# A sparse expert layer on one Trainium2 core: gate and up weights as the stationary operand, fetched per tile through a ring

## The chip, the core and the metric

The kernel runs on one core of a Trainium2 chip. Five engines work side by side, each with its own instruction stream: PE (TensorE, matrix products, with PEld for the loading of its stationary operand), DVE (VectorE), ACT (ScalarE), POOL (GpSimd) and SP (SyncE, which here only issues DMAs). They meet through semaphores. The metric is the device time of one execution in microseconds; lower is better.

## What is computed

Two transformer-like layers over `x` of shape (4, 256, 256). Each layer adds the result of an attention-like block and of an expert block. The change touches only the expert block of layer 0:

```python
x = hidden_states.reshape(-1, 256)                # 1024 tokens
probs = softmax(x @ w_router)                     # 8 experts
top_vals, top_idx = top_k(probs, 2)
for e in range(8):
    w_e = sum(where(top_idx == e, top_vals, 0))   # 0 for most tokens
    g = x @ w_gate[e] * 0.5                       # 256 x 512
    u = x @ w_up[e]                               # 256 x 512
    h = silu(g) * u @ w_down[e] * 0.25            # 512 x 256
    out = out + w_e[:, None] * h
```

## The kernel before

**The stages.** Layer 0's graph attention runs until about 235 us of the span, then the router and the sparse expert stage until about 452 us, then layer 1's graph block, its attention, and its 33 dense experts until the end.

**The sparse stage.** Each token goes to 2 of 8 experts, so there are 2048 (token, expert) rows. They are sorted by expert into tiles of 128 rows, each expert's group filled up to a multiple of 128, which makes TILES = 23 tiles at most. VectorE works out the place of each row (`slot`) and for each tile the expert that owns it, as an offset into the weights (`w_at`). POOL scatters the rows of `norm` to `x_rows` in DRAM with 16 indirect DMAs. SP waits for all of them (`rows_out`) and then loads tile after tile into `xg`, three buffers. After the last tile POOL gathers the results from `y_rows`.

**The weights.** All of gate, up and down of the 8 experts lie in `w_all`, 12.6 MB, loaded at the start of the program by 24 DMAs of 512 KB (L404 to L408). A tile's three weight blocks are addressed by a register that PE loads from `w_at` (`value_load`, L707).

**One tile on PE.** `turn_rows` (L703) transposes the 128 x 256 rows into `XB`, ACT copies them to `xgT` (L966). `gate` (L712) and `up` (L720) take `xgT` as the stationary operand and the weights as the moving one, 512 columns wide, 2 products each; the result has tokens on partitions. ACT makes `gact` = silu (L973), DVE multiplies with the up bank to `hid` (L1455). Because the down product needs the inner index on partitions, `turn_hidden` (L729) transposes `hid` in 4 blocks and ACT copies them to `hgT` (L979). `down` (L737) is 4 products with 256 moving columns. ACT copies the result to `yg` (L985), SP stores it (L460). Products are in float32, of which the trace shows two PE records for each product and one for each transpose.

**The order.** It is written out by hand. In iteration j PE runs gate(j), turn_hidden(j-1), up(j), turn_rows(j+1), down(j-1). On SP the order is store_rows(j), then load_rows(j+3), so that the rows of tile j+3 are fetched only once the result of tile j is copied. DVE uses the time between its products for the top-k search of layer 1's graph block (`keep_top`, L1438 to L1443), 4 steps for each tile. PE's sequencer handles its instructions in order and hands the products to a queue in front of the array; records of that sequencer are shown as PEldq.

Of the kernel before, what the change touches and what calls it, by code (L numbers as in the profile page):

```python
# [14 lines left out]
P = 128  # L15
B, N, D = 4, 256, 256
# [19 lines left out]
O_RING = 6  # L36

# [3 lines left out]
WROW = 3 * GU  # L41
# [54 lines left out]
def build(nc, x, ctxT, W0, W1, a_self0, a_neigh0, a_self1, a_neigh1, b01,  # L96
          w_router, w_gate, w_up, w_down, WqT, WkT, gamma, ln1, ln2, Wq, Wk, Wv, Wo, Wr, ebias,
          Wg, Wu, Wd, ident_in, ind_in, rope_q, rope_k, causal_in, before_in, out):
    with ExitStack() as ctx:
# [88 lines left out]
        w_all = sb_early("w_all", [P, E0, 3, GU])  # L188
# [17 lines left out]
        hgT = sb_sparse("hgT", [P, 2, I0 // P, P])  # L206
# [10 lines left out]
        w_at = sb_sparse("w_at", [P, TILES], I32)  # L217
        last = sb_sparse("last", [P, 2, T])
# [22 lines left out]
        def sb_resting(name, shape):  # L241
# [26 lines left out]
            "x_in", "const_in", "gat_in", "sim_in", "w_all_in", "before_in",  # L268
# [10 lines left out]
            "hid_turned", "hgT_copied", "y_ready", "y_copied", "tok_added", "sig_kept",  # L279
# [99 lines left out]
        def _(sp):  # L379
# [23 lines left out]
            for e in range(E0):  # L403
                sp.dma_start(w_all[:, e, 0, :].rearrange("p (c n) -> p c n", c=HC),  # L404
                             w_gate[e].rearrange("(c p) n -> p c n", p=P)).then_inc(S["w_all_in"], 16)
                sp.dma_start(w_all[:, e, 1, :].rearrange("p (c n) -> p c n", c=HC),
                             w_up[e].rearrange("(c p) n -> p c n", p=P)).then_inc(S["w_all_in"], 16)
                sp.dma_start(w_all[:, e, 2, :].rearrange("p (c n) -> p c n", c=I0 // P),  # L408
                             w_down[e].rearrange("(c p) n -> p c n", p=P)).then_inc(S["w_all_in"], 16)
# [82 lines left out]
        def _(pe):  # L492
# [200 lines left out]
            def sparse_mixture():  # L693
                GB, UB, XB, HB, YB = bank[0:2], bank[2:4], bank[4], bank[5], bank[6:8]
                flat_w = w_all[:].rearrange("p e m n -> p (e m n)")
                ats = {}

                def turn_rows(j):
                    pe.wait_ge(S[f"xg_in{j % 3}"], 16 * (j // 3 + 1))
                    if j >= 2:  # L700
                        pe.wait_ge(S["xgT_copied"], j - 1)
                    for c in range(HC):
                        mm = pe.transpose(XB[:, j % 2 * D + c * P:j % 2 * D + c * P + P], xg[:, j % 3, c * P:c * P + P], ident[:])  # L703
                    mm.then_inc(S["xg_turned"], 1)

                def gate(j):
                    ats[j] = pe.value_load(w_at[0:1, j:j + 1], min_val=0, max_val=(E0 - 1) * WROW)  # L707
                    pe.wait_ge(S["xgT_copied"], j + 1)
                    if j >= 2:
                        pe.wait_ge(S["gact_done"], j - 1)  # L710
                    for c in range(HC):
                        mm = pe.matmul(GB[j % 2][:], xgT[:, j % 2, c, :], flat_w[:, bass.ds(ats[j] + c * I0, I0)],  # L712
                                       start=c == 0, stop=c == HC - 1)
                    mm.then_inc(S["gate_ready"], 1)

                def up(j):
                    if j >= 2:
                        pe.wait_ge(S["hid_done"], j - 1)
                    for c in range(HC):
                        mm = pe.matmul(UB[j % 2][:], xgT[:, j % 2, c, :], flat_w[:, bass.ds(ats[j] + (GU + c * I0), I0)],  # L720
                                       start=c == 0, stop=c == HC - 1)
                    mm.then_inc(S["up_ready"], 1)

                def turn_hidden(j):
                    pe.wait_ge(S["hid_done"], j + 1)
                    if j >= 1:
                        pe.wait_ge(S["hgT_copied"], j)
                    for c in range(I0 // P):
                        mm = pe.transpose(HB[:, c * P:c * P + P], hid[:, j % 2, c * P:c * P + P], ident[:])  # L729
                    mm.then_inc(S["hid_turned"], 1)  # L730

                def down(j):
                    pe.wait_ge(S["hgT_copied"], j + 1)
                    if j >= 2:
                        pe.wait_ge(S["y_copied"], j - 1)
                    for c in range(I0 // P):
                        mm = pe.matmul(YB[j % 2][:, 0:D], hgT[:, j % 2, c, :], flat_w[:, bass.ds(ats[j] + (2 * GU + c * D), D)],  # L737
                                       start=c == 0, stop=c == I0 // P - 1)
                    mm.then_inc(S["y_ready"], 1)

                pe.wait_ge(S["w_all_in"], 16 * 3 * E0)
                pe.wait_ge(S["owner_done"], 1)
                turn_rows(0)
                for j in range(TILES + 1):
                    if j < TILES:
                        gate(j)
                    if j >= 1:
                        turn_hidden(j - 1)
                    if j < TILES:
# [120 lines left out]
        def _(act):  # L870
# [88 lines left out]
            def sparse_mixture():  # L959
                GB, XB, HB, YB = bank[0:2], bank[4], bank[5], bank[6:8]  # L960
# [14 lines left out]
                def copy_hidden(j):  # L975
                    act.wait_ge(S["hid_turned"], j + 1)
                    if j >= 2:
                        act.wait_ge(S["y_ready"], j - 1)
                    act.activation(hgT[:, j % 2].rearrange("p c n -> p (c n)"), HB[:], ACT.Copy).then_inc(S["hgT_copied"], 1)  # L979

# [7 lines left out]
                for j in range(TILES + 1):  # L988
                    if j < TILES:
                        gates(j)  # L990
                    if j >= 1:
# [242 lines left out]
        def _(dve):  # L1234
# [131 lines left out]
            def router0():  # L1366
# [42 lines left out]
                dve.tensor_scalar(w_at[:], owner[:], float(E0 - 1), float(WROW), ALU.min, ALU.mult).then_inc(S["owner_done"], 1)  # L1409
# [36 lines left out]
            def sparse_mixture():  # L1446
# [3 lines left out]
                for j in range(TILES):  # L1450
                    dve.wait_ge(S["gact_done"], j + 1)
                    dve.wait_ge(S["up_ready"], j + 1)
                    if j >= 2:
                        dve.wait_ge(S["hid_turned"], j - 1)
# [316 lines left out]
```

## Time and profile before

| | us |
|---|---|
| median of 3 runs | 1225.0 (1222.7 to 1226.8) |
| the profiled execution | 1225.96 |
| its span, first to last instruction | 1223.9 |
| outside the span | 2.1 |
| PE busy in the span | 1072.3 (88%) |
| DVE busy | 874.4 (71%) |
| ACT busy | 592.0 (48%) |
| POOL busy | 379.0 (31%) |
| mean granted TensorE clock | 0.906 of 2.4 GHz |

"Busy" is a mean over stages with different limits. For this change the stretch from 287.8 us (first product of the sparse stage) to 427.5 us (its last result copied) matters.

### The profile page before, as it was taken

What the parts mean: (1) busy time and instruction counts of PE and PEld (TensorE: products, weight loads), DVE (VectorE), ACT (ScalarE), POOL (GpSimd) and SP (SyncE); (2) the same over time, 40 slices, a digit from 0 to 9 for tenths busy, and PEclk for the clock granted to TensorE, in tenths of its full rate; (3) what the DMA queues carried; (4) which work ended last, traced back from release to release, by engine and by line L of the source; (5) the groups of instructions that cost most, each with busy time, mean ns of one, the idle gap of its engine ahead of it and who ended that gap; (6) DMA issues with size and microseconds to landing.
All of it is one profiled execution on the core that took longest, in us unless ns stands there. A gap on an engine that the chain in (4) does not pass through costs nothing.

```text
span 1223.9 us, 20173 instructions
## 1 busy us (share of the span) xinstructions
PE 1072.3 (88%) x6074; PEld 865.3 (71%) x6074; DVE 874.4 (71%) x2600; ACT 592.0 (48%) x1547; POOL 379.0 (31%) x315
## 2 busy tenths in 40 slices
PE   7988889535999903699999999999997999999998
PEld 3555555332666602599999999999996888888887
DVE  4787776732777348777777777777776887887887
ACT  4656465301333311577777777877775222222221
POOL 0756465122000052433333323322211233233231
PEclk9978776757999955899999999999997999999999
DMA  7900000101111131010101101000000111111111
GB/s 235 363 1 2 1 1 1 63 35 57 43 44 52 36 107 39 24 50 6 36 5 40 36 1 32 2 1 1 2 2 15 51 51 39 51 51 39 51 51 35
DMA packets 55568, 53.56 MB, mean 44 GB/s; under 512 B 5520, under 2 KB 48976, under 8 KB 55488
## 3 DMA queue, kind: packets, MB, share of 16 engines
q1 hardware_dynamic: 53952, 48.38, 12.6%
q0 software_dynamic: 1536, 4.20, 1.1%
q8 instruction: 40, 0.66, 0.2%
q14 instruction: 40, 0.33, 0.1%
HBM read 43.38 MB, written 9.18 MB: 43 GB/s over the span
## 4 chain that ended last, share of the span: by engine, by line
PE 78%; DVE 8%; issue 6%; ACT 4%; POOL 2%; DMA 1%; SPq 1%; DVEq 0%; ACTq 0%; POOLq 0%
PE bank L56 12%; PE bank L57 12%; PE bank L58 12%; PE bank L802 7%; PE bank L823 5%; PE bank L581 4%; PE bank L712 3%; PE bank L812 3%; PE bank L737 3%; PE bank L720 3%; PE bank L564 2%; PE bank L824 2%; DVE g_scale L1319 2%; PE bank L550 2%; PE bank L781 1%
## 5 line engine op out<-in xcount | busy, mean ns | idle before, releaser
L1216 POOL TENSOR_TENSOR rot_s<-swap,rq 128x512 f32<-128x512 f32 x64 | 89.2, 1394 | 196.4 <-ACT swap L1034 196.4
L952 ACT ACTIVATE silu<-bank 128x512 f32<-128x512 f32 x66 | 39.4, 598 | 177.9 <-PE bank L58 177.9
L1643 DVE TENSOR_TENSOR o_ring<-bank,o_ring 128x256 fp32r<-128x256 f32 x128 | 54.3, 424 | 93.6 <-ACT o_ring L1063 92.9
L1047 ACT ACTIVATE prob<-prob,pmin 128x128 f32<-128x128 f32 (+1 forms) x256 | 113.1, 445 | 3.6 <-DVE pmin L1624 3.6
L802 PE MATMUL bank<-kv,norm 128*128 128x128 f32 (+1 forms) x512 | 106.8, 332 | 3.2 <-DVE norm L1617 3.2
L1513 DVE SCALAR_TENSOR_TENSOR xs<-bank,wt,xs 128x256 f32<-128x256 f32 x264 | 109.1, 476 | 0.0
L1162 POOL TENSOR_TENSOR gate_r<-gate_w,gate_r 128x256 fp32r<-128x256 f32 x33 | 38.8, 1175 | 221.5 <-ACT gate_r L938 221.5
L1144 POOL TENSOR_SCALAR rest<-alpha 128x512 f32<-128x512 f32 x32 | 69.3, 2164 | 78.6 <-ACT alpha L884 77.2
L1063 ACT ACTIVATE o_ring<-bank 128x256 fp32r<-128x256 f32 x128 | 48.3, 378 | 82.1 <-PE bank L824 82.0
L56 PE MATMUL bank<-wo_r,o_ring 128*128 128x256 f32 x256 | 84.1, 328 | 0.0
L1624 DVE CUSTOM_DVE_ANT_0 prob<-bank,causal 128x128 f32<-128x128 f32 (+1 forms) x256 | 80.2, 350 | 0.8 <-PE bank L802 0.8
L1636 DVE TENSOR_SCALAR prob<-prob,pinv 128x128 f32<-128x128 f32 (+1 forms) x256 | 76.0, 339 | 4.6
L1492 DVE TENSOR_TENSOR hidf<-silu,bank 128x512 f32<-128x512 f32 x66 | 45.4, 688 | 45.9 <-ACT silu L952 43.6
L823 PE MATMUL bank<-probT,kv 128*128 128x256 f32 x256 | 76.9, 382 | 0.7 <-DVE o_ring L1643 0.7
L56 PE MATMUL bank<-down_r,hidT 128*128 128x256 f32 x264 | 74.7, 283 | 2.0 <-DVE hidT L1497 2.0
L58 PE MATMUL bank<-down_r,hidT 128*128 128x256 f32 x264 | 74.7, 283 | 0.0
L57 PE MATMUL bank<-down_r,hidT 128*128 128x256 f32 x264 | 74.7, 283 | 0.0
L1301 DVE CUSTOM_DVE_ANT_0 alpha<-alpha,norm 128x256 f32<-128x256 f32 x128 | 62.0, 521 | 17.3 <-POOL alpha L1147 16.8
L564 PE MATMUL bank<-ident,alpha 128*128 128x128 f32 x256 | 50.9, 333 | 25.0 <-ACT alphaT L903 14.1
L58 PE MATMUL bank<-wo_r,o_ring 128*128 128x256 f32 x256 | 72.3, 282 | 0.0
L57 PE MATMUL bank<-wo_r,o_ring 128*128 128x256 f32 x256 | 72.2, 282 | 0.0
L802 PEld LDWEIGHTS bank<-kv,norm 128*128 128x128 f32 x512 | 68.8, 195 | 4.0 <-DVE norm L1617 3.6
(240 smaller groups left out, 3116.3 us busy)
## 6 DMA issues: line engine op xcount, KB each, us to landing
gate_w<-in_Wg SPq DMA_DIRECT2D x33, 128.0 KB, 2.1
up_w<-in_Wu SPq DMA_DIRECT2D x33, 128.0 KB, 2.3
down_w<-in_Wd SPq DMA_DIRECT2D x33, 128.0 KB, 2.3
w_all<-in_w_gate SPq DMA_DIRECT2D x8, 512.0 KB, 10.3
w_all<-in_w_up SPq DMA_DIRECT2D x8, 512.0 KB, 10.3
w_all<-in_w_down SPq DMA_DIRECT2D x8, 512.0 KB, 10.3
wq_g<-in_Wq SPq DMA_DIRECT2D x4, 1024.0 KB, 5.0
wo_g<-in_Wo SPq DMA_DIRECT2D x4, 1024.0 KB, 5.4
```

The costliest lines, as they stand in the source:

```text
L56: pe.matmul(out, lhs[0], rhs[0], start=first, stop=False)
L57: pe.matmul(out, lhs[0], rhs[1], start=False, stop=False)
L58: return pe.matmul(out, lhs[1], rhs[0], start=False, stop=last)
L564: mm = pe.transpose(PTB[k % 2][:, mc * N + nt * P:mc * N + nt * P + P], alpha[:, k % RING, nt * N + mc * P:nt * N + mc * P + P], ident[:])
L802: mm = pe.matmul(S_BANK[u % 2][:, nt * P:nt * P + (nt + 1) * P], qT[:, (u // 2) % 4, b2 * N + nt * P:b2 * N + nt * P + P], kT[:, b * N:b * ...
L823: pe.matmul(O_BANK[:, 0:N], vt[:, t, :], probT[:, u % 2, 0:N], start=True, stop=False)
L1047: ins = act.activation(prob[:, u % 4, nt * P:nt * P + (nt + 1) * P], prob[:, u % 4, nt * P:nt * P + (nt + 1) * P], ACT.Exp, bias=pmin[:, u ...
L1144: pool.tensor_scalar(rest[:], alpha[:, k % RING, :], 1.0 / NEG - 1.0, 0.0, ALU.mult, ALU.min).then_inc(S["z_rest"], 1)
L1216: pool.tensor_tensor(rot_s[:, m % 2].rearrange("p (b n) -> p b n", b=2), swap[:, m % 2].rearrange("p (b n) -> p b n", b=2), bcast(tab[:, 1 ...
L1513: ins = dve.scalar_tensor_tensor(xs[:, t, :], DB[2 * (mod % 2) + j // 2][:, j % 2 * D:j % 2 * D + D], w, xs[:, t, :], ALU.mult, ALU.add)
L1624: ins = dve.tensor_tensor_reduce(out=prob[:, u % 4, nt * P:nt * P + (nt + 1) * P], in0=S_BANK[u % 2][:, nt * P:nt * P + (nt + 1) * P], in1 ...
L1636: ins = dve.tensor_scalar(prob[:, u % 4, nt * P:nt * P + (nt + 1) * P], prob[:, u % 4, nt * P:nt * P + (nt + 1) * P], pinv[:, u % 4, nt:nt ...
```

## The change

It turns the roles in gate and up round: blocks of 128 x 128 of the weights are stationary and `xgT` moves, 128 columns wide. The result then has the inner index on partitions, and `hid` can be the stationary operand of down as it is. `turn_hidden`, `copy_hidden` and `hgT` go. Only the down weights stay resident (`w_out`, 8 DMAs of 512 KB at the start); the gate and up weights of a tile's expert are fetched by two DMAs of 512 KB into a ring of three (`w_in`), by the new `load_inner` on SP, with the expert's number read from `e_at`.

```diff
+            def load_inner(j):
+                e = sp.value_load(e_at[0:1, j:j + 1], min_val=0, max_val=E0 - 1)
+                if j >= W_RING:
+                    sp.wait_ge(S["up_ready"], j - W_RING + 1)
+                for m, w in enumerate((w_gate, w_up)):
+                    sp.dma_start(w_in[:, j % W_RING, m, :].rearrange("p (c n) -> p c n", c=HC),
+                                 w[bass.ds(e, 1)].rearrange("e (c p) n -> p (e c) n", p=P)
+                                 ).then_inc(S[f"w_in{j % W_RING}"], 16)
+
+            sp.wait_ge(S["owner_done"], 1)
+            for j in range(W_RING):
+                load_inner(j)
             sp.wait_ge(S["rows_out"], 16 * K0 * T)
             for j in range(3):
                 load_rows(j)
             for j in range(TILES):
+                if j + W_RING < TILES:
+                    load_inner(j + W_RING)
                 store_rows(j)
                 if j + 3 < TILES:
                     load_rows(j + 3)
...
+                def inner(dst, j, m):
+                    for i in range(I0 // P):
+                        for c in range(HC):
+                            mm = pe.matmul(dst[:, i * P:i * P + P], w_in[:, j % W_RING, m, c * I0 + i * P:c * I0 + i * P + P],
+                                           xgT[:, j % 2, c, :], start=c == 0, stop=c == HC - 1)
+                    return mm
...
                 def gate(j):
-                    ats[j] = pe.value_load(w_at[0:1, j:j + 1], min_val=0, max_val=(E0 - 1) * WROW)
+                    pe.wait_ge(S[f"w_in{j % W_RING}"], 32 * (j // W_RING + 1))
                     pe.wait_ge(S["xgT_copied"], j + 1)
...
+                def down(j):
                     pe.wait_ge(S["hid_done"], j + 1)
-                    if j >= 1:
-                        pe.wait_ge(S["hgT_copied"], j)
-                    for c in range(I0 // P):
-                        mm = pe.transpose(HB[:, c * P:c * P + P], hid[:, j % 2, c * P:c * P + P], ident[:])
-                    mm.then_inc(S["hid_turned"], 1)
-
-                def down(j):
-                    pe.wait_ge(S["hgT_copied"], j + 1)
                     if j >= 2:
                         pe.wait_ge(S["y_copied"], j - 1)
-                    for c in range(I0 // P):
-                        mm = pe.matmul(YB[j % 2][:, 0:D], hgT[:, j % 2, c, :], flat_w[:, bass.ds(ats[j] + (2 * GU + c * D), D)],
-                                       start=c == 0, stop=c == I0 // P - 1)
+                    at = pe.value_load(w_at[0:1, j:j + 1], min_val=0, max_val=(E0 - 1) * GU)
+                    for i in range(I0 // P):
+                        mm = pe.matmul(YB[j % 2][:, 0:D], hid[:, j % 2, i * P:i * P + P], flat_w[:, bass.ds(at + i * D, D)],
+                                       start=i == 0, stop=i == I0 // P - 1)
                     mm.then_inc(S["y_ready"], 1)
...
-                pe.wait_ge(S["w_all_in"], 16 * 3 * E0)
+                pe.wait_ge(S["w_out_in"], 16 * E0)
...
-                    if j >= 1:
-                        copy_hidden(j - 1)
```

VectorE gets one instruction more, which writes `e_at` just before `w_at`, and its wait for `hid_turned` becomes one for `y_ready`.

PE, one iteration of the sparse stage before. A row is an instruction with its tiles; `ISA` rows compute register addresses, `TENSOR_LOAD` is the `value_load`.

```order
L707 TENSOR_LOAD w_at
L707 ISA x2
L712 ISA
L712 MATMUL bank<-w_all,xgT 128x512
L712 ISA
L712 MATMUL bank<-w_all,xgT 128x512
L729 MATMUL bank<-ident,hid 128x128 x4
L720 ISA
L720 MATMUL bank<-w_all,xgT 128x512
L720 ISA
L720 MATMUL bank<-w_all,xgT 128x512
L703 MATMUL bank<-ident,xg 128x128 x2
```

The same iteration of PE in the changed kernel (L721 is gate and up, L714 turn_rows, L743 down).

```order
L721 MATMUL bank<-xgT,w_in 128x128 x16
L714 MATMUL bank<-ident,xg 128x128 x2
L741 TENSOR_LOAD w_at
L741 ISA x2
L743 ISA
L743 MATMUL bank<-w_out,hid 128x256
```

The register load stood at the head of gate, right behind down(j-2) in program order. It now stands between the transposes of the new rows and down.

SP, the queue of DMAs in the stage, before and (below) in the changed kernel.

```order
L443 DMA wv_g<-in_Wv 128x2x128
L456 DMA xg<-x_rows 128x256 [waits rows_out]
L456 DMA xg<-x_rows 128x256 x2
L460 DMA y_rows<-yg 128x256 [waits y_copied]
L456 DMA xg<-x_rows 128x256 [waits xg_turned]
```

In the changed kernel L453 loads the rows, L457 stores the result, L465 loads the weights.

```order
L461 TENSOR_LOAD e_at
L461 ISA x2
L465 ISA [waits up_ready]
L465 DMA w_in<-in_w_gate 128x2x512
L465 DMA w_in<-in_w_up 128x2x512
L457 DMA y_rows<-yg 128x256 [waits y_copied]
L453 DMA xg<-x_rows 128x256 [waits xg_turned]
```

Between the load of one tile's rows and the store of the next result SP now also issues 1 MB of weights.

## Rows read from the trace of the kernel before

**Rows 1.** Busy time by stretch: the warm sparse stage, early weight loading (clock, DMA share, GB/s last).

```profile
core 0: us, PE busy (x) PEld busy (x) DVE busy (x) ACT busy (x) POOL busy (x), PEclk, DMA share, GB/s
295.70:423.80 128.10, 128.03 (x484) 79.26 (x485) 88.58 (x263) 39.98 (x86) 0.00 (x0) 1.00 0.14 43
30.00:40.00 10.00, 9.16 (x28) 5.81 (x28) 7.69 (x23) 7.44 (x14) 9.51 (x7) 1.00 1.07 374
```

**Rows 2.** Timeline of PE over one tile: start us, length us, records.

```profile
342.43 1.88 PE L712 MATMUL bank<-w_all,xgT 128*128 x4
344.14 0.60 PE L729 MATMUL bank<-ident,hid 128*128 128x128 f32 x4
344.58 1.88 PE L720 MATMUL bank<-w_all,xgT 128*128 x4
346.30 0.38 PE L703 MATMUL bank<-ident,xg 128*128 128x128 f32 x2
346.52 1.89 PE L737 MATMUL bank<-w_all,hgT 128*128 x8
348.25 1.88 PE L712 MATMUL bank<-w_all,xgT 128*128 x4
```

**Rows 3.** Timeline of PE and PEld around 848 us, float32 products with 128 moving columns.

```profile
847.71 1.95 PE L781 MATMUL bank<-wv_g,actT 128*128 128x128 f32 x16
849.50 0.60 PE L823 MATMUL bank<-probT,kv 128*128 128x256 f32 x2
...
847.50 1.97 PEld L781 LDWEIGHTS bank<-wv_g,actT 128*128 128x128 f32 x16
```

**Rows 4.** Timeline of ACT and SP in the same tile as rows 2, and SP one tile on.

```profile
342.63 0.38 ACT L985 ACTIVATE yg<-bank 128x256 f32<-128x256 f32 x1 [1.34 <-PE bank L737]
...
343.04 0.32 SPq L460 DMA_DIRECT2D y_rows<-yg  x1
343.40 0.43 SPq L456 DMA_DIRECT2D xg<-x_rows  x1
348.86 0.32 SPq L460 DMA_DIRECT2D y_rows<-yg  x1
349.22 1.10 SPq L456 DMA_DIRECT2D xg<-x_rows  x1
```

**Rows 5.** By tile: landing of the xg loads (23), then PE's sequencer in one tile.

```profile
DMA to landing us min/median/max: 2.1/2.2/2.7
...
L735 PEldq EVENT_SEMAPHORE  x1: 51/51/51, 345.6 to 345.6; - x1
```

**Rows 6.** PE's sequencer around the register load of one tile: duration ns, first and last start.

```profile
L707 PEldq TENSOR_LOAD <-w_at x1: 302/302/302, 340.5 to 340.5; - x1
L707 PEldq FUSED_REGOPS  x1: 151/151/151, 340.9 to 340.9; - x1
L707 PEldq SEQ_ASSERT  x1: 18/18/18, 341.1 to 341.1; - x1
...
L710 PEldq EVENT_SEMAPHORE  x1: 51/51/51, 341.2 to 341.2; - x1
```

**Rows 7.** DMA issues: out<-in engine op xcount, KB each, median us to landing.

```profile
wq_g<-in_Wq SPq DMA_DIRECT2D x4, 1024.0 KB, 5.0
```

**Rows 8.** Timeline of the last tile's end.

```profile
421.96 1.89 PE L737 MATMUL bank<-w_all,hgT 128*128 x8
422.22 0.69 DVE L1455 TENSOR_TENSOR hid<-gact,bank 128x512 f32<-128x512 f32 x1 [5.13 <-PE bank L720]
423.69 0.60 PE L729 MATMUL bank<-ident,hid 128*128 128x128 f32 x4
425.06 1.99 PE L737 MATMUL bank<-w_all,hgT 128*128 x8 [0.77 <-ACT hgT L979]
426.88 0.60 PE L764 MATMUL bank<-ident,kv 128*128 128x128 f32 x4
```

**Rows 9.** Timeline of the stage's start and, later, 128 moving columns at half clock.

```profile
289.02 3.78 PE L712 MATMUL bank<-w_all,xgT 128*128 x4 [0.56 <-ACT xgT L966]
292.59 2.41 PE L720 MATMUL bank<-w_all,xgT 128*128 x4
...
485.35 3.38 PE L781 MATMUL bank<-wv_g,actT 128*128 128x128 f32 x16 [0.81 <-ACT actT L1010]
```

**Rows 10.** Timeline: DVE's product and ACT's copy in one tile; POOL's first and last scatter.

```profile
340.85 0.69 DVE L1455 TENSOR_TENSOR hid<-gact,bank 128x512 f32<-128x512 f32 x1 [1.12 <-PE bank L720]
...
263.75 1.22 POOL L1176 DMA_INDIRECT x_rows<-norm,slot  x1 [43.33 <-DVE slot L1405]
...
283.00 0.96 POOL L1176 DMA_INDIRECT x_rows<-norm,slot  x1 [0.30 <-issue]
```

More of the change, by code:

```diff
@@ L36 @@
 O_RING = 6
+W_RING = 3
 SLOTS = B * N * K0
@@ L187, in build @@
         g_pos = sb_early("g_pos", [P, 2, N])
-        w_all = sb_early("w_all", [P, E0, 3, GU])
+        w_out = sb_early("w_out", [P, E0, GU])
+        w_in = sb_early("w_in", [P, W_RING, 2, GU])
         early.close()
@@ L217, in build @@
         w_at = sb_sparse("w_at", [P, TILES], I32)
+        e_at = sb_sparse("e_at", [P, TILES], I32)
         last = sb_sparse("last", [P, 2, T])
@@ L403, in _ @@
             for e in range(E0):
[L404 to L409, printed above, removed]
+                sp.dma_start(w_out[:, e, :].rearrange("p (c n) -> p c n", c=I0 // P),
+                             w_down[e].rearrange("(c p) n -> p c n", p=P)).then_inc(S["w_out_in"], 16)
             def load_expert(which, e, par):
@@ L693, in sparse_mixture @@
             def sparse_mixture():
-                GB, UB, XB, HB, YB = bank[0:2], bank[2:4], bank[4], bank[5], bank[6:8]
-                flat_w = w_all[:].rearrange("p e m n -> p (e m n)")
-                ats = {}
+                GB, UB, XB, YB = bank[0:2], bank[2:4], bank[4], bank[6:8]
+                flat_w = w_out[:].rearrange("p e n -> p (e n)")
                 def turn_rows(j):
@@ L710, in gate @@
                         pe.wait_ge(S["gact_done"], j - 1)
[L711 to L714, printed above, removed]
+                    inner(GB[j % 2], j, 0).then_inc(S["gate_ready"], 1)
                 def up(j):
@@ L718, in up @@
                         pe.wait_ge(S["hid_done"], j - 1)
[L719 to L724, printed above, removed]
-                    pe.wait_ge(S["hid_done"], j + 1)
-                    if j >= 1:
-                        pe.wait_ge(S["hgT_copied"], j)
-                    for c in range(I0 // P):
-                        mm = pe.transpose(HB[:, c * P:c * P + P], hid[:, j % 2, c * P:c * P + P], ident[:])
-                    mm.then_inc(S["hid_turned"], 1)
-                def down(j):
-                    pe.wait_ge(S["hgT_copied"], j + 1)
+                    inner(UB[j % 2], j, 1).then_inc(S["up_ready"], 1)
+                def down(j):
+                    pe.wait_ge(S["hid_done"], j + 1)
                     if j >= 2:
                         pe.wait_ge(S["y_copied"], j - 1)
-                    for c in range(I0 // P):
-                        mm = pe.matmul(YB[j % 2][:, 0:D], hgT[:, j % 2, c, :], flat_w[:, bass.ds(ats[j] + (2 * GU + c * D), D)],
-                                       start=c == 0, stop=c == I0 // P - 1)
+                    at = pe.value_load(w_at[0:1, j:j + 1], min_val=0, max_val=(E0 - 1) * GU)
+                    for i in range(I0 // P):
+                        mm = pe.matmul(YB[j % 2][:, 0:D], hid[:, j % 2, i * P:i * P + P], flat_w[:, bass.ds(at + i * D, D)],
+                                       start=i == 0, stop=i == I0 // P - 1)
                     mm.then_inc(S["y_ready"], 1)
-                pe.wait_ge(S["w_all_in"], 16 * 3 * E0)
+                pe.wait_ge(S["w_out_in"], 16 * E0)
                 pe.wait_ge(S["owner_done"], 1)
@@ L746, in sparse_mixture @@
                         gate(j)
-                    if j >= 1:
-                        turn_hidden(j - 1)
-                    if j < TILES:
                         up(j)
@@ L959, in sparse_mixture @@
             def sparse_mixture():
[L960 removed]
+                GB, XB, YB = bank[0:2], bank[4], bank[6:8]
                 def copy_rows(j):
@@ L973, in gates @@
                     act.activation(gact[:, j % 2, :], GB[j % 2][:], ACT.Silu, scale=0.5).then_inc(S["gact_done"], 1)
[L975 to L979, printed above, removed]
                 def copy_out(j):
@@ L1408, in router0 @@
                 chain.link(dve.tensor_reduce(owner[:], ends[:], X, ALU.add))
-                dve.tensor_scalar(w_at[:], owner[:], float(E0 - 1), float(WROW), ALU.min, ALU.mult).then_inc(S["owner_done"], 1)
+                dve.tensor_scalar(e_at[:], owner[:], float(E0 - 1), None, ALU.min)
+                dve.tensor_scalar(w_at[:], owner[:], float(E0 - 1), float(GU), ALU.min, ALU.mult).then_inc(S["owner_done"], 1)
                 for k, test in enumerate((ALU.is_equal, ALU.not_equal)):
```

9 lines of the change are left out of this document (3 added, 6 removed).

## The prediction

> **What bounds the kernel now.** I read the busy shares by stretch first, then PE's timeline over one tile, then what ACT, SP and PE's sequencer do in that tile. From 295.7 to 423.8 us PE is busy 128.03 of 128.10 us at the full granted clock, 2.4 GHz [rows 1]: the sparse stage is bound by PE, without gaps. Taking start to start, one tile is gate 1.71, turn_hidden 0.44, up 1.72, turn_rows 0.22 and down 1.73 us, together 5.82 [rows 2]. Everything else fits under that. DVE and ACT have idle time before each tile's work (1.12 us before the product, 1.34 before the copy) [rows 4, 10]. The DMAs use 0.14 of their time [rows 1]. But one loop is nearly as long as PE's. The rows of tile j+3 are asked for only when the result of tile j is copied. In the tile that starts at 342.43 the copy runs from 342.63, the store is issued at 343.04, the rows' load at 343.40 [rows 2, 4]. With a landing of 2.2 us that is 345.6, and at 345.6 PE's sequencer is at L735, the first instruction behind the transposes that need these rows [rows 5]. I read this as the sequencer having stood at the wait for that DMA. PE itself reaches the transposes at 346.30 [rows 2], so the cover is 0.7 us.
>
> **The change, part by part.**
>
> Gate and up. Each was 2 products of 512 columns and becomes 8 of 128, the same columns in all. The nearest row is L781, float32, 128 moving columns, a new stationary block for each record: 16 records from 847.71 to the next product at 849.50, 0.112 us each [rows 3]. A product is two records, so gate takes 16 x 0.112 = 1.79 us and up the same, +0.15 us a tile for both.
>
> Here a rule of the Trainium skill speaks against the change. The row says that 16 loads take 1.97 us beside 16 products that take 1.95 [rows 3]: the loads run under the products. The page "TensorE: Matmul & The Clock Gate", Part 3, says that a weight load overlaps a product in flight only if it goes to other row groups, and these blocks use all rows; its Part 2 also allows a load into a background buffer. If loads were added to products, the case is rival D.
>
> turn_hidden and copy_hidden. 4 transposes go, -0.44 us of PE a tile [rows 2]. ACT loses a 0.6 us copy that nobody waited for, except at the end.
>
> PE's own sum is then 1.79 + 1.79 + 0.22 + 1.73 = 5.53 us a tile, 0.29 less than 5.82. If that were all, 22 tiles would give -6.4 us.
>
> The register load. It moves from the head of gate, where 1.73 us of queued down products covered it, to between turn_rows and down. So it now stands behind the wait for the DMA, where the cover is gone. From its start to the next instruction of the sequencer is 340.5 to 341.2, 0.7 us [rows 6]. With about 0.1 us for the semaphore instruction before it and 0.1 for the address and first block after it, down's first product can start 0.9 us after the rows land. Counted from the start of gate: rows land at 345.6 - 342.43 = 3.17, down can start at 3.17 + 0.9 = 4.07. PE would be ready for it at 1.79 + 1.79 + 0.22 = 3.80, so it idles 0.27 us. Restarted after such a gap, 8 down records take 425.06 to 426.88, 1.82 us [rows 8]. The tile takes 4.07 + 1.82 = 5.89 us, and the next copy, store and load hang on its end: the round result, copy, store, load, sequencer, down is the new bound, 0.07 us longer than PE's 5.82 before. This holds for the iterations 2 to 21, in which the rows come by that round: 20 x 0.07 = +1.4 us.
>
> The own size of the register load is a second place for the skill. The row has 302 ns for the load alone [rows 6]. The page "DMA: Bandwidth & Descriptors", Latency and other measured facts, gives a floor of about 600 ns for it. By the page each tile would be 0.3 us longer and the sum 6 us higher; the trace does not agree here, and its duration is used.
>
> The late issue. One rows' load of the 21 in the loop took 1.10 us to issue instead of 0.43 (at 349.22) [rows 4]. The cover took it before; now it lands in full: +0.6 us. SP issues twice as many DMAs, and such an issue may come oftener, up to three times, +1.2 more at the upper bound.
>
> The 1 MB of weights a tile. Behind the rows' load, SP is free at 1.40 us after the start of gate (343.40 + 0.43). Its register load is 0.8 us by the same rows [rows 6]; the two DMAs start to issue at 2.2. A DMA of 1 MB lands 5.0 us after its issue [rows 7], so this lands at 7.2, that is 1.3 us into the next tile, and is wanted more than one tile later. Its data stop moving some time before that landing. The next store is issued at 0.6 and the next rows' load at 1.0 into that tile, and a load of 128 KB needs 2.2 us of which little is data, at 374 GB/s (1 MB in 2.8 us) [rows 1, 5]. So I take no delay. The bounds are zero and half of the 1 MB still ahead of the rows, 1.4 us a tile; nearest to zero because the transfer has 5.9 us for 2.8 us of work. The range keeps a part of it. A gain from it is excluded, since nothing waited for these weights.
>
> The start. `load_inner` for tiles 0 to 2 waits for `owner_done`, which comes near the first scatter at 263.75; the last scatter is issued at 283.00 [rows 10]. 3 MB are 8.4 us, done before. VectorE's additional instruction stands behind `slot_done`, on which the scatters hang, so it costs nothing. At half clock 16 records of 128 columns take 3.38 us (ends included), gate's four before took 3.57 start to start [rows 9]: even. The down weights still come in long before. The 8 MB less at the start had no one waiting.
>
> The ends. Iterations 1 and 22 lose the 0.29 us: -0.6. After the last down-but-one, PE turned `hid`, waited for ACT's copy and started down at 425.06, 1.37 us after 423.69 [rows 8]. Now `hid` is ready at 422.22 + 0.69 = 422.91, the register load and address make it 423.8, against 423.69: about 0.15 of the 1.37 stays, and with the restart at 0.1 the gain is -1.1 us.
>
> Sum: +1.4 + 0.6 - 0.6 - 1.1 = +0.3 us. The profiled execution had 1225.96, which gives 1226.3; the median of the runs is 1.0 below it, which gives 1225.3.
>
> **The rivals.**
>
> B, the register load stays covered. If the sequencer does not stand at the DMA's wait but runs on (L735 at 345.6 would then be chance), or rows land 0.3 us earlier than I read, PE's 5.53 holds: 22 x -0.29 - 1.1 = -7.5 us, 1217.5. For it: the queue before PE is evidently long, since the sequencer is at L707 at 340.5, nearly 2 us before gate starts. Against it: the agreement of landing and L735.
>
> C, the weights stand before the rows in the DMA engines. In place is SP's one queue: the 1 MB of one tile is issued before the next store and rows' load. It decides once the last bytes of the 1 MB move later than about 2 us into the next tile; my reckoning has them end at about 1. Each 0.1 us past that costs 2 us in all, since the round has no cover left. With 0.4 us a tile the time is 1225.3 + 8 = 1233; with the full 1.4 us it is 1253. For it: the round is now the bound, so every delay of issue or landing counts, and landings went up to 2.7 us even with an idle queue [rows 5]. The slower register load belongs here by its size.
>
> D, weight loads are not hidden for 128 columns: each record costs 0.112 more, 32 x 0.112 x 23 = +82 us, 1307. The row of L781 speaks against it [rows 3].
>
> That the new form leaves PE with the old 5.82 because it does not do what it says is excluded by the instruction order.
>
> **How the numbers follow.** Within 0.3% (3.7 us, about what a measurement of this kernel can tell from no change) around 1225.0 is my forecast, the round as the bound: 0.53, its own range 1222 to 1229. B, faster by more than 0.3%: 0.18. C, slower: 0.27; D: 0.02. Predicted is 1225.3. The range reaches down to B's 1217 and up to 1236, which leaves out the larger half of C's sizes and D, about 0.15. Faster 0.18, same 0.53, slower 0.29.
>
> **What would show it.** In the changed kernel's profile: L721 records 0.112 us apart at full clock (right), 0.2 and more (D). Start of gate to start of gate 5.9 us with a gap of about 0.3 us on PE before each down, from tile 2 on (right); 5.5 without gap (B); 6.2 and more with xg landings above 2.4 us (C). The sequencer's register load should start at the landing of xg. The gap between the last two downs shrinks from 1.4 us to about 0.2. If the store or rows' load is issued later than 0.6 and 1.0 us after the start of gate, SP's queue was the error. It would be wrong altogether if the granted clock fell in the stage because of the gaps, which no row suggests.

## The result and the profile after

The changed kernel takes 1231.9 us (median of 8 runs, 1228.6 to 1232.7) against 1225.9 for the kernel before in the same session: ratio 1.0050, 95% interval 1.0035 to 1.0064. It is slower, by 6 us. The prediction said 1225.3, "within 0.3%" as the likeliest case; the time lies inside the whole range given (1217 to 1236) and outside the likeliest case's own range (1222 to 1229). The profiled execution took 1230.93 us against 1225.96, so the profile shows 5.0 of the 6 us.

The busy time by stretch comes first, as in [rows 1]; the columns are the same.

```profile
core 0: us, PE busy (x) PEld busy (x) DVE busy (x) ACT busy (x) POOL busy (x), PEclk, DMA share, GB/s
295.70:426.80 131.10, 125.41 (x911) 115.32 (x910) 87.17 (x259) 29.23 (x64) 0.00 (x0) 1.00 0.59 202
310.00:410.00 100.00, 94.95 (x680) 86.52 (x680) 70.58 (x210) 22.20 (x49) 0.00 (x0) 1.00 0.63 214
```

Before, PE was busy 128.03 of 128.10 us. Now it idles 5.7 us of 131.1, at the same full clock, and the DMAs carry 202 GB/s instead of 43. PE is no longer the bound. Why the idle time is there shows in two kinds of tile. The first kind is the tile forecast: PE's timeline over tile and end of stage (it answers to [rows 2] and [rows 8]), SP's timeline in the same tile, and then the register loads of PE's sequencer (ns min/median/max).

```profile
417.22 3.73 PE L721 MATMUL bank<-xgT,w_in 128*128 128x128 f32 x32
420.80 0.38 PE L714 MATMUL bank<-ident,xg 128*128 128x128 f32 x2
421.29 1.99 PE L743 MATMUL bank<-w_out,hid 128*128 x8
423.12 3.73 PE L721 MATMUL bank<-xgT,w_in 128*128 128x128 f32 x32
426.69 3.71 PE L743 MATMUL bank<-w_out,hid 128*128 x16
430.24 0.60 PE L767 MATMUL bank<-ident,kv 128*128 128x128 f32 x4
...
417.83 0.34 SPq L457 DMA_DIRECT2D y_rows<-yg  x1
418.23 0.42 SPq L453 DMA_DIRECT2D xg<-x_rows  x1
...
L741 PEldq TENSOR_LOAD <-w_at x23: 295/302/506, 296.9 to 427.7; - x23
```

Gate and up together are 3.58 us, the rows' load is issued 1.01 us after the start of gate, and down starts at 4.07 us, although the transposes were done at 3.80. The tile takes 5.90 us. These are the prediction's 3.58, 1.0, 4.07, 3.80 and 5.89.

The second kind was not forecast at this frequency. PE's timeline of the tile that starts at 342.50, then SP's. Brackets hold the idle time before a row and what ended it.

```profile
342.50 3.73 PE L721 MATMUL bank<-xgT,w_in 128*128 128x128 f32 x32
346.45 0.44 PE L714 MATMUL bank<-ident,xg 128*128 128x128 f32 x2 [0.21 <-DMA xg<-x_rows]
347.31 1.99 PE L743 MATMUL bank<-w_out,hid 128*128 x8 [0.42 <-issue]
349.13 3.73 PE L721 MATMUL bank<-xgT,w_in 128*128 128x128 f32 x32
355.23 3.73 PE L721 MATMUL bank<-xgT,w_in 128*128 128x128 f32 x32
...
343.11 0.34 SPq L457 DMA_DIRECT2D y_rows<-yg  x1
343.51 1.38 SPq L453 DMA_DIRECT2D xg<-x_rows  x1
345.63 0.40 SPq L465 DMA_DIRECT2D w_in<-in_w_gate  x1
346.13 0.41 SPq L465 DMA_DIRECT2D w_in<-in_w_up  x1
349.74 0.34 SPq L457 DMA_DIRECT2D y_rows<-yg  x1
350.14 0.43 SPq L453 DMA_DIRECT2D xg<-x_rows  x1
```

The rows' load starts on time, 1.01 us after gate, but takes 1.38 us to issue instead of 0.43. The rows land 2.9 us after the start of the issue instead of 2.2, so 0.7 us late; PE waits first for them and then for its sequencer, and the tile takes 6.63 us. The tile behind it, 349.13 to 355.23, still has 6.10. The tile view of xg gives the issue over all tiles (ns min/median/max) and the landing:

```profile
L453 SPq DMA_DIRECT2D xg<-x_rows x23: 343/425/1386, 284.7 to 418.2; - x23
...
DMA to landing us min/median/max: 2.0/2.2/3.1
```

Of the 20 periods of the loop, six hold such an issue (0.9 to 1.39 us): 6.59, 6.63, 6.51, 6.88, 6.54 and 6.21 us, and two stand behind one (6.10 and 6.37). The others lie between 5.81 and 5.96.

What stands beside the late issues is in the view of the DMA queues (packets, MB, share of 16 engines over the stretch). The first stretch is 343.2 to 343.8, around the late issue. The second is the 0.4 us before the one late issue of the kernel before, at 349.22 [rows 4].

```profile
q1 hardware_dynamic: 24, 0.03, 13.2%
q8 instruction: 1, 0.02, 12.5%
```

```profile
q8 instruction: 1, 0.02, 19.4%
```

Queue q8 fetches instructions, 16 KB in one packet. They are PE's: in a run below, 45 more instructions on PE moved four of the seven fetches in the loop one tile ahead. 12.5% of 16 engines over 0.6 us is 1.2 us for the packet. In the trace of the changed kernel each of the six late rows' loads (and a weights' load of 1.30 us at 309.2) has such a fetch beside it and is released about 0.4 us after the fetch ends. Fetches come every 13 to 19 us instead of every 23 to 29, since a tile now has 42 product records on PE and had 22. The experiments ask how much each of these two findings, the bare round and the late issue, is worth.

The stage was also measured alone, from the start of the first gate product to the first transpose behind the last down:

| kernel | stage, us | against before | rest of the span behind it |
|---|---|---|---|
| before | 137.86 | | 797.0 |
| after | 142.16 | +4.3 | 798.9 |
| after, again | 144.31 | +6.5 | 796.7 |
| after with 45 more PE instructions ahead | 143.23 | +5.4 | 798.3 |
| early register load | 134.10 | −3.8 | 796.6 |
| rows first | 130.15 | −7.7 | 797.1 |
| both | 129.92 | −7.9 | 798.0 |
| no reload of weights | 139.41 | +1.6 | 799.0 |
| half of the weights | 138.43 | +0.6 | 796.2 |
| two register loads | 153.65 | +15.8 | 798.1 |
| products of before, weights by ring | 138.48 | +0.6 | 799.5 |
| before with rows first | 137.98 | +0.1 | 797.1 |

The last column moves over 3.3 us in no relation to the edits, so what one profile shows behind the stage (+1.9 here) is scatter of single executions. The stage column carries the argument, but it scatters too: two profiles of the changed kernel differ by 2.1 us. The medians of the runs agree with the column to within about 2 us. One run of the kernel with the products of before and weights by ring took 1442.2 us and is left out of its median.

### The profile page after: what moved, and what is told of

Read it like the earlier page. It is cut to its first block, busy times and chain, and to the rows that moved or that the text cites. A ratio compares the mean times of both kernels' runs of the same rounds, so it can differ in the third digit from the quotient of the medians.

```text
span 1229.1 us, 21098 instructions
## 1 busy us (share of the span) xinstructions
PE 1073.5 (87%) x6526; PEld 908.1 (74%) x6534; DVE 874.6 (71%) x2601; ACT 580.7 (47%) x1524; POOL 379.6 (31%) x315
## 4 chain that ended last, share of the span: by engine, by line
PE 78%; DVE 9%; issue 4%; ACT 4%; DMA 2%; POOL 2%; SPq 1%; DVEq 0%; ACTq 0%; POOLq 0%
PE bank L56 13%; PE bank L57 12%; PE bank L58 12%; PE bank L805 7%; PE bank L721 6%; PE bank L826 4%; PE bank L593 4%; PE bank L743 4%; PE bank L815 3%; PE bank L576 2%; PE bank L827 2%; DVE g_scale L1314 2%; PE bank L562 2%; PE bank L784 1%; POOL ytok L1179 1%
## 5 line engine op out<-in xcount | busy, mean ns | idle before, releaser
L721 PEld LDWEIGHTS bank<-xgT,w_in 128*128 128x128 f32 x736 | 87.9, 196 | 2.8 <-issue 1.7
L721 PE MATMUL bank<-xgT,w_in 128*128 128x128 f32 x736 | 88.3, 280 | 1.1 <-ACT xgT L969 1.1
L56 PE MATMUL bank<-wo_r,o_ring 128*128 128x256 f32 x256 | 84.2, 329 | 0.0
L58 PE MATMUL bank<-wo_r,o_ring 128*128 128x256 f32 x256 | 72.3, 283 | 0.0
```

What stands on the lines that cost most here:

```text
L56: pe.matmul(out, lhs[0], rhs[0], start=first, stop=False)
L58: return pe.matmul(out, lhs[1], rhs[0], start=False, stop=last)
L721: mm = pe.matmul(dst[:, i * P:i * P + P], w_in[:, j % W_RING, m, c * I0 + i * P:c * I0 + i * P + P], xgT[:, j % 2, c, :], start=c == 0, st ...
```

## The experiments

Each was timed beside the kernel before; times are medians, ratios are against the kernel before with their 95% intervals. The kernel before had medians of 1225.1, 1225.7 and 1224.9 us in the three sessions; a ratio can differ by 0.001 from that of two medians.

**The register load back ahead of gate.**

```diff
 def gate(j):
+    ats[j] = pe.value_load(w_at[0:1, j:j + 1], ...)
     pe.wait_ge(S[f"w_in{j % W_RING}"], 32 * (j // W_RING + 1))
 ...
 def down(j):
-    at = pe.value_load(w_at[0:1, j:j + 1], ...)
+    at = ats[j]
```

> The changed kernel with one thing moved: PE's register load for down (302 ns, 0.7 us with what follows it) stands at the head of gate again, as in the kernel before. Theory (the round result, copy, store, rows' load, register load, down closes the loop): down can start as soon as the rows have landed and the transposes are done, so a tile takes PE's own 3.57 + 0.22 + 1.72 = about 5.55 us instead of 5.89, there is no gap before down except in tiles whose rows' load is issued late, and the time falls by about 20 x 0.34 = 7 us against the changed kernel, plus some 2 us of late issues that the regained 0.3 us of cover take: 1222 to 1225. Rival (the 1 MB of weights a tile is what slows the rows): the gaps stay, 1230 to 1232.

Measured 1221.4 us, 0.9960 (0.9943 to 0.9977). PE's timeline has both kinds of tile again:

```profile
367.03 0.44 PE L715 MATMUL bank<-ident,xg 128*128 128x128 f32 x2 [0.52 <-DMA xg<-x_rows]
367.30 1.92 PE L745 MATMUL bank<-w_out,hid 128*128 x8
369.06 3.73 PE L722 MATMUL bank<-xgT,w_in 128*128 128x128 f32 x32
372.63 0.38 PE L715 MATMUL bank<-ident,xg 128*128 128x128 f32 x2
372.85 1.89 PE L745 MATMUL bank<-w_out,hid 128*128 x8
374.58 3.73 PE L722 MATMUL bank<-xgT,w_in 128*128 128x128 f32 x32
```

369.06 to 374.58 is 5.52 us with PE never idle: the new products are 0.3 us a tile cheaper, once the register load is covered. 13 of 20 tiles are so. Where the rows' load is issued late (up to 1.60 us here), PE still waits for the rows, 0.5 us in the tile shown. The place of the register load is therefore worth 8 us of stage in the profiles and about 10 us by the medians, a little more than expected, and the late issues survive.

**Rows before result on SP.**

```diff
     load_inner(j + W_RING)
-store_rows(j)
 if j + 3 < TILES:
     load_rows(j + 3)
+store_rows(j)
```

> The changed kernel with SP's order turned: the rows of tile j+3 are loaded before the result of tile j is stored, so that they no longer wait for its copy. The register load stays where the change put it. Theory (the round through SP is the bound): the rows are there a tile ahead, PE's sequencer never stands at their wait, the register load is hidden by the queued products, every tile takes about 5.55 us, and the late issues no longer reach PE: against the changed kernel -7 us for the gaps and -5 us for the late issues, 1218 to 1220. Rival (the register load costs PE its 0.7 us wherever it stands before down): the tile stays at 5.8 or more, 1228 and above.

Measured 1217.9 us, 0.9929 (0.9904 to 0.9954), faster than both kernels by more than the intervals, and with the next run the fastest of all. Busy time in the middle of the stage, then PE's and SP's timeline:

```profile
310.00:410.00 100.00, 100.00 (x765) 96.29 (x764) 75.84 (x226) 24.98 (x55) 0.00 (x0) 1.00 0.68 238
...
368.99 3.73 PE L721 MATMUL bank<-xgT,w_in 128*128 128x128 f32 x32
374.51 3.73 PE L721 MATMUL bank<-xgT,w_in 128*128 128x128 f32 x32
...
366.16 0.46 SPq L453 DMA_DIRECT2D xg<-x_rows  x1
369.60 0.34 SPq L457 DMA_DIRECT2D y_rows<-yg  x1
370.70 0.95 SPq L465 DMA_DIRECT2D w_in<-in_w_gate  x1
371.75 0.41 SPq L465 DMA_DIRECT2D w_in<-in_w_up  x1
372.22 0.46 SPq L453 DMA_DIRECT2D xg<-x_rows  x1
```

The rows' load no longer waits for the result's copy, so there is no round. It is issued right behind the 1 MB of weights and lands only after 4.3 us (median; 5.0 at most), twice as long as before, and nobody waits: all tiles are 5.52 us. Late issues are there too (0.95 us at 370.70 is one), and cost nothing. The stage is 7.7 us shorter than before; rival B of the prediction had priced exactly this state, PE's own sum, at 7.5.

**Both edits.** 

> The changed kernel with both corrections, the register load at the head of gate and the rows' load ahead of the store. Theory: with the rows first PE has no gap left (5.52 us a tile in all 20), so the register load's place is worth nothing more: the same as e2, 1217 to 1219, ratio to the kernel before 0.991 to 0.995. Rival (the register load still costs PE something): 1 us or more below e2.

Measured 1218.8 us, 0.9945 (0.9924 to 0.9966), stage 129.92 against 130.15. The second edit adds nothing to the first: with rows early, the register load is covered again where it stands.

**The same order in the kernel before.** The two lines on SP exchanged in the kernel before. 

> The kernel before with SP's order turned as in e2: rows of tile j+3 loaded before the result of tile j is stored. Theory: PE had no gaps there, so nothing changes, 1224.5 to 1226, ratio 0.999 to 1.001. Rival (the earlier loads help by themselves, so that the gain of e2 is not the form of the products): 1222 or less.

Measured 1226.4 us, 0.9999 (0.9983 to 1.0016); all tiles 5.82, PE busy 100.00 of 100 us. The time is 0.4 us above the range expected, the ratio inside it. The kernel before gains nothing from it, since PE bounded it. The gain of the kernel above is that of the change, freed of its round.

**Two register loads.**

```diff
+pe.value_load(w_at[0:1, j:j + 1], ...)
 at = pe.value_load(w_at[0:1, j:j + 1], ...)
```

> The changed kernel with PE's register load in front of down done twice. Theory (it stands bare between the landing of the rows and down): the second one adds its full 0.65 to 0.7 us to each of the 20 tiles in the loop, +13 to +14 us against the changed kernel, 1244 to 1246, and the tile's period goes from 5.9 to 6.55. Rival (it is covered and something else makes the gap): no more than 2 us are added.

Measured 1242.5 us, 1.0139 (1.0111 to 1.0167).

```profile
368.01 3.73 PE L721 MATMUL bank<-xgT,w_in 128*128 128x128 f32 x32
371.58 0.38 PE L714 MATMUL bank<-ident,xg 128*128 128x128 f32 x2
372.91 1.99 PE L744 MATMUL bank<-w_out,hid 128*128 x8 [0.95 <-issue]
374.74 3.73 PE L721 MATMUL bank<-xgT,w_in 128*128 128x128 f32 x32
```

Down now starts 4.90 us after gate instead of 4.07, and most tiles take 6.6 us, 0.7 more than the 5.9. That shows each register load bare on the round, at the 0.7 us of [rows 6]. The total is 1.5 us under the range expected, and only one late issue (0.94 us) is in this profile, although the same 1 MB of weights moves in every tile. The tile is 0.7 us longer, so the weights' bytes end earlier against the next gate. Here is q8 from 327.7 to 328.1 in the tile that starts at 327.80, then the rows' load:

```profile
q8 instruction: 1, 0.02, 16.1%
...
328.80 0.42 SPq L453 DMA_DIRECT2D xg<-x_rows  x1
```

The fetch starts with gate and takes 1.0 us, where six of the seven in the changed kernel's loop start 0.6 to 1.1 us behind it. Five of the seven fetches in the loop lie so, from 0.2 us before gate to 0.1 behind it, and delay the rows' load by at most 0.1 us. Of the other two, one makes the late issue, and the other starts 0.4 us behind the issue of a load that then landed after 2.8 us (its tile took 7.25).

**No weights in the loop.** The tiles from the fourth on use the weights of the first three.

```diff
-if j + W_RING < TILES:
-    load_inner(j + W_RING)
 store_rows(j)
 ...
-pe.wait_ge(S[f"w_in{j % W_RING}"], 32 * (j // W_RING + 1))
+pe.wait_ge(S[f"w_in{j % W_RING}"], 32)
```

> The changed kernel without the weight loads of tiles 3 to 22: the ring keeps the weights of the first three tiles, so most tiles are computed with another tile's gate and up weights; all instructions of PE, ACT and DVE are the same. It takes away 20 MB of traffic and 40 DMAs from SP's queue. Theory A (the late issues of the rows' load in 6 of 20 tiles come from the fetch of PE's instructions, 16 KB at a time, which starts within 0.5 us of each of them): they stay, and the time is that of the changed kernel, 1230 to 1232. Theory B (they come from the weights' descriptors in the same queue, or from their bytes still moving): they go, the tiles take 5.9 us throughout, 4 to 5 us less, 1226 to 1228.

Measured 1226.8 us, 1.0005 (0.9987 to 1.0024). My theory had expected 1230 to 1232, with the late issues still there. It fell; the rival's number came.

```profile
366.09 3.73 PE L719 MATMUL bank<-xgT,w_in 128*128 128x128 f32 x32
372.00 3.73 PE L719 MATMUL bank<-xgT,w_in 128*128 128x128 f32 x32
376.00 0.44 PE L712 MATMUL bank<-ident,xg 128*128 128x128 f32 x2 [0.26 <-DMA xg<-x_rows]
...
372.62 0.32 SPq L457 DMA_DIRECT2D y_rows<-yg  x1
372.98 1.35 SPq L453 DMA_DIRECT2D xg<-x_rows  x1
```

366.09 to 372.00 is 5.91 us: the round is as long without any traffic of weights, so it is made of waits and not of contention. But only two of 20 tiles suffer now (6.71 and 6.67): the one shown, and one whose load was issued in time and landed after 3.0 us, with a fetch that started 0.6 us behind it. PE's instructions are as many as in the changed kernel, and the fetches too. What differs is their place in the tile: five of the seven in the loop begin 0.7 to 1.0 us before the result's store is issued, and are over when the rows' load is. In the changed kernel six of them begin between 0.04 us before and 0.45 us after the store's issue, and are in the way of the rows' load.

**The products of the kernel before, with the weights fetched for each tile.**

```diff
-for i in range(I0 // P):
-    for c in range(HC):
-        mm = pe.matmul(dst[:, i * P:i * P + P], w_in[...], xgT[:, j % 2, c, :], ...)
+for c in range(HC):
+    mm = pe.matmul(GB[j % 2][:], xgT[:, j % 2, c, :], w_in[:, j % 3, 0, c * I0:c * I0 + I0], ...)
 ...
+turn_hidden(j - 1)
```

> The kernel before with the ring alone: gate and up weights are fetched per tile as in the change, but they move and xgT is stationary as before, with turn_hidden, and the register load at the head of gate. Theory (the traffic itself costs nothing; what costs is the lost cover): a tile takes 5.82 us, as before, and longer only where a rows' load is issued more than 0.7 us late, 0 to 2 us in all: 1225 to 1228. Rival (1 MB a tile delays the rows or slows PE's reads): 1230 and above.

Measured 1226.9 us, 0.9997 (0.9978 to 1.0016). The issues of rows reach 1.61 us here too, and five in the loop are late (0.79 us and more), but most of this is covered: three tiles have 6.10, 6.37 and 5.94 us and the others 5.82. In the profile the DMA ring alone costs 0.6 us of stage. Weights, fetches and late issues do harm only by what goes beyond the cover of the round.

**The changed kernel again, and with 45 more instructions on PE ahead of the stage.** The added instructions only raise a semaphore; they shift the boundaries of the 16 KB blocks to other instructions.

```diff
+for _ in range(45):
+    pe.sem_inc(S["pe_held"])
 pe.wait_ge(S["w_out_in"], 16 * E0)
```

> The changed kernel itself once more, on the same chip as the next three, so that they have it beside them. Both theories: 1230 to 1232 where the kernel before has 1225 to 1226, and the same 6 or 7 late issues, since the fetches of PE's instructions stand at fixed places of its program.

> The changed kernel with 45 semaphore increments more in PE's program, just before the sparse stage, where PE waits anyway; everything else is the same, the 1 MB of weights a tile too. It moves every later 16 KB piece of PE's instructions by 45 instructions, about half a tile. Theory A (the rows' load is issued late when it falls into the fetch of such a piece): the fetches fall elsewhere in the tile, late issues go from 7 to 3 or fewer in the profile, and the time falls by 2 to 4 us against the changed kernel, with the other tiles still at 5.9. Theory B (late issues come from the weights' traffic): 6 or 7 late issues and no change.

Measured 1232.1 us, 1.0043 (1.0026 to 1.0060), and 1232.1 us, 1.0046 (1.0028 to 1.0063). The first profile has seven late issues in the loop. The second has six, and a seventh load that was issued in time and landed after 3.2 us, with a fetch 0.5 us behind it. Four of the seven fetches fall one tile earlier with the added instructions, but again behind the start of gate, by 0.4 to 0.8 us (one by 1.5) against 0.5 to 1.0. So the place of a block's end among the instructions doesn't decide where in the tile a fetch runs; the expectation that the shift would change the number of late tiles fell.

**Half of the weights.** Only the gate weights are fetched, and up computes with them too. The DMA wait takes half the count.

```diff
-for m, w in enumerate((w_gate, w_up)):
+for m, w in enumerate((w_gate,)):
```

> The changed kernel with only the gate weights fetched, 512 KB a tile instead of 1 MB; up is computed with the gate weights too, by the same instructions. The padded run left the fetches of PE's instructions at the same time of the tile, 0.6 to 1.0 us after the start of gate, which is when the weights' bytes end; with no weights at all the fetches came 0.1 to 0.4 us before it. Theory C (such a fetch is asked for a little before the start of gate and stands behind the weights' bytes; it then falls on the rows' load that SP issues at 1.0): with half of the bytes, which end some 1.4 us earlier, the fetches start near -0.4 again, at most 2 rows' loads are issued late, and the time is that of the run without weights, 1226 to 1228. Rival D (the number of DMAs or any traffic at all is what counts): 5 to 7 late issues as before, 1230 to 1232, or in between in proportion.

Measured 1225.4 us, 1.0003 (0.9981 to 1.0026). First q8 in the stretch from 324.1 to 324.5, then PE and SP there:

```profile
q8 instruction: 1, 0.02, 15.1%
```

```profile
324.42 3.73 PE L721 MATMUL bank<-xgT,w_in 128*128 128x128 f32 x32
...
325.03 0.32 SPq L457 DMA_DIRECT2D y_rows<-yg  x1
325.39 0.43 SPq L453 DMA_DIRECT2D xg<-x_rows  x1
```

The fetch takes 15.1% of 16 x 0.4 us, 1.0 us, and starts ahead of gate. The rows' load that follows at 325.39 is issued in 0.43 us. In the changed kernel, the tile that starts at 324.16 has its fetch start at 324.9 and its rows' load take 1.16 us. With half the bytes one rows' load in the loop is late by much (1.50 us) where six were, and its stage is 3.7 us shorter. The time is a little under the range expected. From none to half the traffic changes little (139.4, 138.4), from half to all it costs 4 to 6 us, by either profile of the changed kernel. The amount of traffic alone is not what decides, since two register loads left all of it in place and had one late issue; both runs fit with the time at which the bytes end. In the changed kernel the 2 KB packets of the weights still move in the first 0.7 us of gate:

```profile
q1 hardware_dynamic: 117, 0.24, 101.6%
```

That is the stretch from 349.2 to 349.8, right behind the start of gate at 349.13: 117 packets, all but one of 2 KB, and the engines full. From 349.9 on they are nearly empty. I read it so that a fetch that was due in this time runs behind these bytes, at 0.6 to 1.1 us, and there meets the rows' load. Two times in each kernel bear on it. Both are medians, in us from the start of gate: the end of the last 2 KB packet, over 19 tiles, and the start of the fetch, over the fetches in the loop (seven; five in the last kernel).

| kernel | ordinary tile, us | bytes end | fetch starts |
|---|---|---|---|
| no reload of weights | 5.9 | none | −0.2 |
| half of the weights | 5.9 | −0.45 | −0.1 |
| two register loads | 6.6 | 0.2 | 0.0 |
| after | 5.9 | 0.9 | 0.8 |
| early register load | 5.52 | 1.3 | 1.1 |
| after, again | 5.85 | 0.9 | 0.8 |
| after with 45 more PE instructions ahead | 5.9 | 0.8 | 0.7 |
| rows first | 5.52 | 0.7 | 1.0 |
| products of before, weights by ring | 5.82 | 1.25 | 0.8 |

The first five rows rise together; the last two do not lie on their line, so the end of the bytes is not all that sets the start of a fetch.

All twelve profiles together say more about the fetch and the issue. 59 loads on SP, of rows or weights, were issued from 0.2 us before a fetch to its end; 58 were released between 0.27 and 0.44 us after the fetch's end, nearly all at 0.37, whether the issue took 0.4 or 1.5 us in all. Of the 550 other loads in the stage two took more than 0.5 us, and one of these was issued 0.2 us before a fetch. The 38 stores that met a fetch took no more than 0.34 us.

## Why the prediction was right, and where it was wrong

| term of the sum | forecast, us | measured in the profile, us |
|---|---|---|
| 20 tiles, the round as bound | +1.4 | +1.5 |
| late issues of the rows' load | +0.6 (up to +1.8) | +4.7 |
| first and last tiles | −1.7 | −1.9 |
| stage | +0.3 | +4.3 |

The time forecast was 6.6 us too low. The whole range held because it kept room for rival C, whose mechanism is not the one that came; that part is luck.

**What bounds the kernel.** Right. The reading that PE's sequencer stood at the rows' DMA with 0.7 us of cover left [rows 5] carried the forecast. Moving the register load behind that wait used the cover up: 5.52 us a tile when it is ahead of gate, 5.90 behind the wait, 6.6 when it is doubled.

**Gate and up.** Right: 3.58 us for both, 0.112 us a record, as L781 had shown [rows 3]. The weight loads are hidden, against what Part 3 of the Trainium skill's page "TensorE: Matmul & The Clock Gate" would give for blocks that use all rows; rival D is out.

**The round.** Right to 0.01 us in the tile at 417.22, by each step. The twelve ordinary tiles take 5.895 us on average, which over 20 is +1.5 us. Rival B's condition, a covered register load, did not hold, and its price was confirmed by rows first (−7.7 us against −7.5).

**The register load's own time.** 302 ns, median of 23, as in [rows 6], and not the 600 ns that the Trainium skill gives on "DMA: Bandwidth & Descriptors", Latency and other measured facts. Two register loads showed that its whole price is the 0.7 us with the address behind it.

**The late issue.** This is the term that was mis-sized. The prediction took one in 21 (the loop has 20 such loads), put at 0.6 us, and up to three times as many, because SP issues twice as many DMAs. Six came, at 0.3 to 1.0 us each, with 0.2 and 0.5 us in two tiles behind them, together +4.7 us. The reasoning had the wrong cause: not SP's number of DMAs, which was as large with two register loads and one late issue, but the fetches of PE's instructions, more of them and later in the tile. They stand beside every late issue, in the kernel before too. The prediction never asked what ran in the DMA queues at 349.22 [rows 4], and took the one late issue for chance.

**The 1 MB of weights.** Half right. The rows were not behind the weights: where their load is issued in time in the loop, it lands after 2.1 to 2.4 us, and did after 2.1 to 2.3 before. The engines are full with their bytes until 0.7 us into the next tile, about where the prediction had them end, and not past the 2 us that rival C needed. C's sign, tiles of 6.2 us and more with landings above 2.4, did show in the six tiles with a late issue; the sign could not tell a late issue from a slow transfer. But the sum took the effect of the traffic as zero, and taking it away or halving it gave 3 to 6 us of stage back. By the reading above it works through something that the prediction did not name: it pushes the fetches of instructions onto the rows' load. C's price of 1233 was near the result for another reason.

**The ends and the start.** Right in sum. From the start of the last down that has no cover to the next transpose it was 4.92 us before (421.96 to 426.88, [rows 8]) and is 3.55 now (426.69 to 430.24): −1.37, for which −1.1 was forecast. The rest of the first and last tiles gave −0.5 for −0.6.

**The chances.** The round without cover was known, and each 0.1 us of further delay priced at 2 us; a resource that was seen once and not explained deserved more than 0.6 us with that price. "Slower" had 0.29 and should have had more than "same".

**What stays open.** That the fetch holds the issue rests on the constant distance between the ends of the two in twelve profiles; no run changes the fetch alone. That the weights' bytes push the fetch back rests on the runs in which the bytes end earlier or later, by less traffic or by a longer or shorter tile. Why a fetch on q8 delays a load on SP's queue and never a store, no run here shows. The new products with the expert's weights resident, without the ring, were not tried.

## What to carry to other kernels

Before an instruction is moved behind a wait on its engine's sequencer, look for the closed round that runs through that wait and measure its cover: here 0.7 us of register load against 0.7 us of cover turned a cheaper tile into a dearer one. Where the round has no cover, each irregular delay in it counts in full, so explain the single odd row of the profile before it is priced as chance. Often the repair is to take a link out of the round: the rows' load didn't need to follow the result's store on SP, and exchanging two lines made +0.5% into −0.7%.

## What the runs showed of the hardware

PE's instructions come in blocks of 16 KB, each one DMA packet of 0.9 to 1.6 us (median 1.0) on a queue of its own. The Trainium skill gives the blocks of 16 KB too ("Runtime: NRT & Kernel Launch", Instruction fetch mechanics), and calls the cost of crossing one mostly hidden. Here it was not: a load issued on SP that meets such a fetch is released 0.37 us after the fetch ends, so it takes up to 1.6 us to issue instead of 0.43, while a store that meets one takes its usual 0.34. Five loads that were issued in time, 0.2 to 0.6 us before a fetch, landed after 2.8 to 3.2 us instead of 2.2. The blocks do not wait for PE to run dry; PE itself never stopped for them in the rows-first kernel, 100.00 of 100 us busy.

An order that looks worse for a load can be the better one: behind 1 MB of weights the rows land after 4.3 us instead of 2.2, and with that order no tile waits.
